# Low halves of the expert weights on GpSimd in quarters, dequantisation in quarters, and new orders of the stages

## The reference

```
x = x + tanh(g) * cross_attention_A(layernorm(x), ctx)   # 4 heads of 64, rotary, 120 context rows
x = x + tanh(g) * fp4_ffn(layernorm(x))                  # 704 hidden, blockwise FP4 quantise + dequantise
x = x + tanh(g) * cross_attention_B(layernorm(x), ctx)   # 16 heads of 16
x = x + tanh(g) * moe_ffn(layernorm(x))                  # 8 experts, top 2, 1024 hidden
```

## Time and profile before

| | us |
|---|---|
| median of 3 runs (1751.59 to 1757.57) | 1753.04 |
| the profiled execution's own time | 1752.59 |
| its span, first to last instruction | 1751.0 |
| busy: PE, DVE, ACT, POOL | 1444.2, 1150.0, 910.7, 595.4 |
| DVE line 1175 (low halves), 48 of 1.216 us | 58.4 |
| POOL line 582 (high halves), 48 of 1.095 us | 52.1 |

### The profile page before, as it was taken

How to read it: one execution, slowest core, us unless ns; L and a number is a source line. 1 busy time by engine, 2 the same in 40 slices (tenths; PEclk the granted TensorE clock), 3 DMA queues, 4 the chain that set the end, 5 groups by cost and what they waited for, 6 DMA issues and landing times.

```text
span 1751.0 us, 36348 instructions
## 1 busy us (share of the span) xinstructions
PE 1444.2 (82%) x12061; PEld 1110.5 (63%) x12062; DVE 1150.0 (66%) x2878; ACT 910.7 (52%) x2701; POOL 595.4 (34%) x704
## 2 busy tenths in 40 slices
PE   2335798898888988898888767199999999999994
PEld 1223565665656665665655444188888888888884
DVE  5657788988889888988888652344444444444442
ACT  1112377677666767677666555144445444455442
POOL 0002233343424433343423320234444334344342
PEclk9556799999999999999999988599999999999997
DMA  5002211222022211222022000554223231132124
GB/s 180 9 0 84 85 35 64 97 97 82 17 97 97 97 37 61 97 97 82 17 88 88 13 7 7 199 180 113 34 32 107 35 105 33 33 105 34 32 30 120
DMA packets 63333, 123.62 MB, mean 71 GB/s; under 512 B 14130, under 2 KB 52140, under 8 KB 59052
## 3 DMA queue, kind: packets, MB, share of 16 engines
q1 hardware_dynamic: 45915, 102.75, 17.0%
q0 software_dynamic: 17312, 19.56, 6.8%
HBM read 78.64 MB, written 48.04 MB: 72 GB/s over the span
## 4 chain that ended last, share of the span: by engine, by line
PE 51%; DVE 28%; ACT 7%; issue 6%; POOL 5%; DMA 1%; SPq 0%; DVEq 0%; ACTq 0%; POOLq 0%
PE bank L1312 13%; PE bank L1314 13%; PE bank L1313 13%; PE bank L1388 3%; DVE b_mn L1047 2%; ACT b_ex L710 2%; POOL f_z L567 2%; PE bank L1401 2%; DVE wm L1125 1%; POOL f_z L565 1%; DVE wm L1117 1%; DVE r_pick L1219 1%; PE bank L1424 1%; DVE a_t L1037 1%; POOL slots L595 1%
## 5 line engine op out<-in xcount | busy, mean ns | idle before, releaser
L1312 PE MATMUL bank<-split_room,wm 128*128 128x256 f16 x1152 | 315.5, 274 | 8.2 <-issue 6.8
L1313 PE MATMUL bank<-split_room,wm 128*128 128x256 f16 x1152 | 315.4, 274 | 0.0
L1314 PE MATMUL bank<-split_room,wm 128*128 128x256 f16 x1152 | 315.3, 274 | 0.0
L1289 DVE SCALAR_TENSOR_TENSOR split_room<-bank,b12e,split_room 128x256 f32<-128x256 f32 x288 | 138.1, 483 | 267.2 <-ACT split_room L833 260.1
L710 ACT ACTIVATE b_ex<-bank,b_mn 128x120 f32<-128x120 f32 x512 | 177.4, 360 | 130.0 <-DVE b_mn L1047 121.1
L833 ACT ACTIVATE split_room<-bank,b12e 128x256 f32<-128x256 f32 x288 | 134.1, 470 | 197.1 <-PE bank L1314 193.7
L656 POOL DMA_INDIRECT acc<-split_room,m_cur x72 | 115.3, 1601 | 132.5 <-ACT split_room L847 105.7
L1314 PE MATMUL bank<-wm,split_room 128*128 128x256 f16 x576 | 157.0, 273 | 0.0
L1313 PE MATMUL bank<-wm,split_room 128*128 128x256 f16 x576 | 157.0, 273 | 0.0
L1312 PE MATMUL bank<-wm,split_room 128*128 128x256 f16 x576 | 157.0, 273 | 0.0
L1388 PE MATMUL bank<-b_k,b_q 128*128 128x480 f32 x256 | 129.1, 586 | 13.9 <-ACT b_q L782 13.9
(11 more groups left out here) (358 smaller groups left out, 3841.8 us busy)
## 6 DMA issues: line engine op xcount, KB each, us to landing
split_room<-in_L_ffn_W SPq DMA_DIRECT2D x48, 512.0 KB, 8.1
wsplit<-split_room SPq DMA_DIRECT2D x16, 1536.0 KB, 6.4
wm<-wsplit SPq DMA_DIRECT2D x16, 1536.0 KB, 8.6
acc<-x SPq DMA_DIRECT2D x17, 256.0 KB, 6.8
xin<-in_x SPq DMA_DIRECT2D x16, 256.0 KB
rows<-r_row SPq DMA_DIRECT2D x16, 256.0 KB, 2.1
ct<-in_ctx SPq DMA_DIRECT2D x16, 120.0 KB
cb<-in_ctx SPq DMA_DIRECT2D x16, 120.0 KB, 5.2
```

Source lines behind the costliest of these rows:

```text
L1289: dve.scalar_tensor_tensor(m_h[:, c % 3], bank[c % 4][:, TILE:2 * TILE], b12e[:, p, 1, c:c + 1], m_s[:, c % 2], ALU.add, ALU.mult).then_in ...
L1312: pe.matmul(o, lh, rh, start=start, stop=False)
L1313: pe.matmul(o, ll, rh, start=False, stop=False)
L1314: return pe.matmul(o, lh, rl, start=False, stop=stop)
```

## The change

On POOL the stage of a chunk now writes the high half in four pieces of 256 columns, waits for its own semaphore, and writes the low half in four pieces too. DVE's three weight stages are gone. `dequantise` does each of its two operations in four pieces (176 columns of 704, or 128 of 512). All engine orders but SP's are written anew.

```
-                pool.tensor_tensor(v, v, m, ALU.subtract).then_inc(F.pool, 1)
+                w = v.shape[1] // PIECES          # PIECES = 4
+                cut = [slice(i * w, (i + 1) * w) for i in range(PIECES)]
+                for c in cut:
+                    last = pool.tensor_tensor(v[:, c], v[:, c], m[:, c], ALU.subtract)
+                last.then_inc(F.pool, 1)
                 pool.wait_ge(F.pool, b * 3 + n + 1)
-                pool.tensor_tensor(blocks(v), blocks(v), over(scale, BLK), ALU.mult).then_inc(F.hq, 1)
+                for c in cut:
+                    sc = scale[:, c.start // BLK:c.stop // BLK]
+                    last = pool.tensor_tensor(blocks(v[:, c]), blocks(v[:, c]), over(sc, BLK), ALU.mult)
+                last.then_inc(F.hq, 1)
...
-                    pool.tensor_scalar(w_hl[:, j, 0], w_st[:, j], 1.0, 1.0, ALU.mult, ALU.mult).then_inc(W.hi, 1)
+                    cut = [slice(i * 256, (i + 1) * 256) for i in range(4)]
+                    for c in cut:
+                        last = pool.tensor_scalar(w_hl[:, j, 0, c], w_st[:, j, c], 1.0, 1.0, ALU.mult, ALU.mult)
+                    last.then_inc(W.hi, 1)
+                    pool.wait_ge(W.hi, b * 3 + j + 1)
+                    for c in cut:
+                        last = pool.tensor_tensor(w_hl[:, j, 1, c], w_st[:, j, c], w_hl[:, j, 0, c], ALU.subtract)
+                    last.then_inc(W.split, 1)
...
-            def weights(j):                       # on DVE
-                def stage(b, p):
-                    dve.wait_ge(W.hi, b * 3 + j + 1)
-                    dve.tensor_tensor(w_hl[:, j, 1], w_st[:, j], w_hl[:, j, 0], ALU.subtract).then_inc(W.split, 1)
-                return stage
```

The orders, new:

```
+            "POOL": ("W0/0 B.ln/2 A.ln/-1 W1/0 R.ln/3 F.p0/1 W2/0 F.p1/1 F.ln/0 R.scatter/3 F.p/0").split(),
+            "ACT": ("F.ht0/2 B.s3/3 A.s0/0 B.t3/3 B.s4/3 F.ht1/2 B.s5/3 B.t4/3 B.s6/3 B.r3/3 F.z/1 A.s1/0 A.t0/0 B.t5/3 "
+                "A.t1/0 B.o0/3 B.s7/3 B.t6/3 B.t7/3 F.t/1 B.r7/3 B.o1/3 A.ot/0 F.gu0/1 F.gu1/1 F.gu2/1 B.z/2 B.ct/2 "
+                "B.zt/2 F.gu3/1 A.z/-1 B.k/2 B.q/2 A.t/-1 R.z/3 R.t/3 B.s0/2 R.logit/3 B.s1/2 B.t0/2 B.s2/2 B.t1/2 B.t2/2").split(),
+            "DVE": ("B.s2/3 F.q1c/2 A.r0/0 A.r1/0 B.s3/3 F.ht0/2 A.s0/0 B.s4/3 B.s5/3 F.ht1/2 B.s6/3 F.ln/1 A.s1/0 B.rx0/3 "
+                "B.p3/3 F.q/1 B.o0/3 B.s7/3 F.d1/2 A.p0/0 B.rx1/3 A.p1/0 F.t/1 B.p7/3 B.ln/2 B.o1/3 A.ot/0 F.gu0/1 "
+                "A.out/0 A.ln/-1 F.gu1/1 B.out/3 F.q0a/1 F.gu2/1 B.ct/2 B.zt/2 R.ln/3 F.gu3/1 F.q0b/1 F.q1a/1 F.q0c/1 "
+                "A.t/-1 F.q1b/1 B.s0/2 R.t/3 B.v/2 R.logit/3 A.rk/-1 B.s1/2 R.rank/3").split(),
+            "PE": ("A.s0/0 B.p1/3 B.t3/3 B.s4/3 B.p2/3 F.ht1/2 B.s5/3 B.t4/3 B.s6/3 A.s1/0 A.t0/0 B.p3/3 F.d0/2 B.p4/3 "
+                "B.t5/3 A.t1/0 B.s7/3 F.d1/2 B.t6/3 B.p5/3 A.p0/0 A.p1/0 B.t7/3 F.t/1 B.p6/3 A.ot/0 B.p7/3 F.gu0/1 "
+                "B.out/3 A.out/0 F.gu1/1 F.gu2/1 B.ct/2 B.zt/2 F.gu3/1 B.k/2 B.q/2 A.t/-1 B.s0/2 R.t/3 A.kv/-1 B.v/2 "
+                "R.logit/3 A.q0/-1 B.s1/2 B.t0/2 R.rank/3 B.s2/2 F.ht0/1 B.p0/2 B.t1/2 A.q1/-1 B.t2/2 B.s3/2").split(),
```

More of the change, by code:

```diff
@@ L35 @@
 QUAD = 4
+PIECES = 4
 HL = 33
@@ L367, in gated_stack @@
             "SP": ("A.load/-1 W/0 B.out/3 B.load/0 R.rank/3").split(),
[L368 to L371, removed]
[3 rows of a table removed]
-                "F.gu2/1 B.zt/2 R.logit/3 A.t/-1 F.gu3/1 F.q0b/1 F.q1a/1 F.q0c/1 R.rank/3 B.s0/2").split(),
[3 rows of a table removed]
-                "A.t/-1 R.logit/3 F.gu3/1 B.k/2 B.q/2 R.rank/3 A.kv/-1 B.s0/2 B.v/2 B.s1/2 A.q0/-1").split(),
+            "POOL": ("W0/0 B.ln/2 A.ln/-1 W1/0 R.ln/3 F.p0/1 W2/0 F.p1/1 F.ln/0 R.scatter/3 F.p/0").split(),
+            "ACT": ("F.ht0/2 B.s3/3 A.s0/0 B.t3/3 B.s4/3 F.ht1/2 B.s5/3 B.t4/3 B.s6/3 B.r3/3 F.z/1 A.s1/0 A.t0/0 B.t5/3 "
+                "A.t1/0 B.o0/3 B.s7/3 B.t6/3 B.t7/3 F.t/1 B.r7/3 B.o1/3 A.ot/0 F.gu0/1 F.gu1/1 F.gu2/1 B.z/2 B.ct/2 "
+                "B.zt/2 F.gu3/1 A.z/-1 B.k/2 B.q/2 A.t/-1 R.z/3 R.t/3 B.s0/2 R.logit/3 B.s1/2 B.t0/2 B.s2/2 B.t1/2 B.t2/2").split(),
[3 rows of a table added]
+                "A.t/-1 F.q1b/1 B.s0/2 R.t/3 B.v/2 R.logit/3 A.rk/-1 B.s1/2 R.rank/3").split(),
[3 rows of a table added]
+                "R.logit/3 A.q0/-1 B.s1/2 B.t0/2 R.rank/3 B.s2/2 F.ht0/1 B.p0/2 B.t1/2 A.q1/-1 B.t2/2 B.s3/2").split(),
         }
@@ L1242, in _ @@
                       "B.ln": variances(B, cb_, F), "B.zt": b_zt_, "B.ct": b_ct_, "B.v": b_v_, "B.p3": b_p_(0), "B.p7": b_p_(1), "B.rx0": b_rx_(0), "B.rx1": b_rx_(1), "B.o0": b_o_(0), "B.o1": b_o_(1), "B.out": add_out(B, x3, x2, bank[4]),
-                      "R.ln": variances(R, cr, B), "R.t": r_t, "R.logit": r_logit, "R.rank": r_rank,
-                      "W0": weights(0), "W1": weights(1), "W2": weights(2)}
+                      "R.ln": variances(R, cr, B), "R.t": r_t, "R.logit": r_logit, "R.rank": r_rank}
             stages.update(ra)
```

## The result

The changed kernel took 1821.8 us (median of 4 runs, 1820.75 to 1824.21) against 1754.9 of the kernel before beside it: ratio 1.0384, 95% interval 1.0372 to 1.0397. It is 67 us slower; 1723 had been forecast.

What follows compares the result with a forecast made beforehand. PE and DVE were taken to share the limit of a 56.1 us step; half of PE's 4.2 us of named waits, 2.1, times 14 gave 29 us off 1752.6, hence 1723, range 1696 to 1760.

Steps and rivals of the forecast that it cites:

- What bounds the kernel: First phase's 56.1 us step: PE and DVE share the limit, neither full; the chain runs mostly on DVE, outside the low halves.
- the sum: Whole first phase: 2.1 us saved a step, times 13 steps and one more for the ramps, 29 us.
- Low halves, pieces, port: Weight work on DVE and POOL: DVE falls to 45.8 us a step, POOL rises to 35, port blocking stays near 3.0.
- the sum over squared lengths: DVE's blocking on the port shared with POOL: price follows POOL's squared instruction lengths, 3.0 us a step instead of 3.3.
- Rival (2): DVE's SBUF port: blocking by POOL eats the 3.65 us relief, so time stays 1753, within 5; chance 0.15.
- The orders: Engine orders: the same stages shuffled, R.rank behind B.s1, so PE's waits of 1.1 and 1.6 us should go.
- PE's named waits of 4.2 us: PE inside one step: waits for exponentials 1.6, router's input 1.1, rotary sum 0.9, f_z 0.6; half the total counted as gain.
- The 1.6 us that R.rank's move was to give: First score round: with R.rank no longer ahead of it on DVE, PE's 1.6 us wait for the exponentials could go.
- F.p1 late: POOL's stretch from F.p0 to F.p1, over 15.4 us, delays F.ht1 on PE by 2.3 us a step: 1785; chance 0.17.
- I cost it at nothing: SP's store and the loads before POOL's W0: issued some 25 us ahead in the new order, so no wait was priced.

Runs made afterwards that it cites:

- e1: The changed kernel's low halves on POOL and its pieces, but with the orders of the kernel before: 1757.4 us.
- e3: As e1, but every POOL operation in one instruction instead of four: 1802.3 us.
- e15: e8 with R.ln on POOL moved ahead of A.ln and W1: 1744.1 us.
- e10: The kernel before with POOL's dequantisation and high halves cut in four, except f_z, left whole; low halves on DVE, old orders: 1723.7 us.
- e13: e10 with DVE's W1 also moved from behind F.d1 to behind A.ot: 1715.1 us.
- e7: e1 with one DVE move, R.rank from in front of B.s0 to behind B.s1: 1780.3 us.
- e8: e1 with POOL's new order alone, the other engines' orders old: 1859.3 us.
- e6: The kernel before with POOL's dequantisation and high halves cut in four, low halves whole on DVE, old orders: 1755.3 us.
- e5: The changed kernel with B.ct, B.zt, B.k and B.z put back between the F.gu stages, only half as in the old orders: 1855.4 us.
- e11: e6 with six additional unread transpositions on PE ahead of its wait for f_z: 1740.1 us.
- e18: e7 with R.logit on ACT moved from in front of B.k to behind B.s0: 1753.9 us.

## Why the prediction was wrong

- **What bounds the kernel.** Right that neither engine was full, that the chain runs through DVE's long stretch, and that none of the low halves is in it. e1 agrees: 3.65 us a step off DVE, and no gain with the old orders. One count was off: with lags from -1 to 3 and 16 blocks, all stages run in steps 3 to 14, 12 of them and not 13, which is 2 us of the sum.
- **Low halves, pieces, port.** Right in the sizes of the work: 0.673 against 0.73 a piece, POOL 33.5 against 35 a step, DVE 45 against 45.8. The port was priced too high: the sum over squared lengths gave 3.0 us a step, and the same three lines in the changed kernel have 2 x (0.613 - 0.424) + 2 x (0.177 - 0.166) + (0.233 - 0.218) = 0.4 us above what the prediction took as their own work. Rival (2), that the port gives all back, describes e3 rather than the change: uncut, the same work costs 45 us more. The warning of the Trainium skill (Perfetto Trace Analysis, Optimizing Scalar/DVE Operations) that such a shift might not help fits e1 and e3, and no run shows the shift itself gaining: e15, all low halves on POOL, is 10 us faster than before, but e10 and e13, which leave them on DVE and cut POOL's work (e13 also moves one stage), are 31 and 39 us faster. What paid was the cutting, which the prediction thought of as the means to the shift. Low halves on POOL together with f_z whole and e15's order of POOL were not run.
- **The orders: this step failed.** "Of PE's named waits of 4.2 us all could go ... I give back half." Of the 4.2, 2.4 went. But new waits of 6.2 us came, so that PE stands 3.8 us more a step, not 2.1 less, and is 1.2 us longer busy, most of it at half the clock (6 falls of 1.7 us each between 280 and 900 us). The 1.6 us that R.rank's move was to give came to 0.3 by itself (e7): the wait went from the first score round to the third. The working priced the stages that were moved away from a wait and none that was moved into one. What it could have read from the two lists: F.gu1 and F.gu2 side by side on PE, the second of which waits until ACT and DVE have taken the first's product, with B.ct, B.zt and R.t gone from between them; B.z on ACT behind F.gu2; and on DVE F.q1b and the router's stages crowded about the first score rounds. In the old order each of these chains had another block's work under it.
- **The rivals.** The slower side was given 0.20 and one mechanism, F.p1 late. Its condition came true and its consequence did not: in the changed kernel POOL takes from 526.1 to 545.0 us from F.p0's start to F.p1's end, 18.9 us where 15.4 was to decide, and PE does not wait at F.ht1; in e8 it waits 0.9 us a step. The time came out of the range's upper end, 1760, by 62 us. The range was made of what the parts might cost and had no term for some 150 entries set anew.
- **"I cost it at nothing"**, of SP's and POOL's new places: right for the loads, wrong for R.ln behind A.ln and W1. By e8 and e15 that place costs 115 us unless the router's stages are late on every engine, and their being late is part of the loss.
- **The clock** was in no term. The kernel before shows none of its falls between 280 and 900 us, and that is luck of its waits: e6, with less waiting in all (4.9 us a step against 6.1), had 22 us of them.

What stays open: why the small swaps of the first half cost 19 us (not divided further), and what makes one wait of 1.6 us bring the clock down and another not. The kernel before has waits of 1.6 to 2.1 us without a fall.

## What to carry to other kernels

In a pipeline of in-order engines a new order is a change of its own: for each stage moved, look for the chained pair that it stood between, and price the pair bare. Test the parts under the old order first (e1, e6), then move one stage at a time; here the best version (e13) is the old order with one stage moved, POOL's work cut but for f_z, and the low halves left where they were. When a run comes out slower, part its difference into PE's waits and PE's busy time before naming a wait as the cause: e5 and e7 lost 33 and 23 us with no more waiting than the kernels that they came from. Where one engine's stage grows fourfold, what stands behind it on that engine (R.ln) matters more than its sum of busy time.

## What the runs showed of the hardware

- TensorE's granted clock dropped to half for 3.4 us (or twice that) after waits of 1.65 to 2.5 us in an otherwise busy stretch (e5, e6, e7), beginning 1.5 us after the wait's end in e6, about at its end in e7, and either way in e5. Each drop of 3.4 us cost 1.7. Filling part of the wait with idle transpositions (e11) kept it at 1.00 and gained 15 us. Splitting a wait of 2.5 us in two of 0.9 and 1.4 (e18) kept it at 1.00 too and gained 26.
- DVE's r_pick, r_w and rotary sum stand while a POOL instruction runs, and get in between two of them. With POOL's work cut in four and the orders kept, the means fell: r_pick from 0.782 us (e3) to 0.278 (e1), the rotary sum from 1.002 to 0.589. It works against POOL too: four pieces took 2.90 us instead of 1.86 with DVE's low half of 1.22 us among them (e6).
- ACT's table load of 1.28 us comes twice a step, with the first Silu after an exponential and the first exponential after a Silu (the two functions alternate in every step). Moving the second from in front of B.k into the first score round (e7, e18) did not lengthen PE's waits: 5.5 and 5.6 us a step.
